# VectorE alone sums the sixteen tiles of expert rows of the first block, one strided reduce for each

## What is computed

```python
x = x + 0.5 * ffn(layernorm(x))
x = x + attn(layernorm(x))
x = x + 0.5 * ffn(layernorm(x))
```

```python
y = jnp.einsum('ecf,edf->ecd', jax.nn.silu(g) * u, down_w)
out = jnp.zeros_like(flat).at[tok_table.reshape(-1)].add((y * w_table[..., None]).reshape(-1, d))
```

## Time and profile before

| | us |
|---|---|
| median of 3 runs | 972.84 (972.01 to 973.99) |
| the profiled execution | 972.94 |
| its span in the trace | 971.2 |

### The profile page before, as it was taken

How to read it: one execution, slowest core, us unless ns; L and a number is a source line. 1 busy time by engine, 2 the same in 40 slices (tenths; PEclk the granted TensorE clock), 3 DMA queues, 4 the chain that set the end, 5 groups by cost and what they waited for, 6 DMA issues and landing times.

```text
span 971.2 us, 18502 instructions
## 1 busy us (share of the span) xinstructions
PE 915.0 (94%) x5770; PEld 561.1 (58%) x5772; DVE 763.6 (79%) x2079; ACT 646.6 (67%) x1426; POOL 645.6 (66%) x607
## 2 busy tenths in 40 slices
PE   4999789999999999999999999999999999978987
PEld 3766466555555555555555555555555555765666
DVE  6954399998888888888888888888878789876247
ACT  5634446877778687777778778777777787543431
POOL 3368778878676868778676766867677455236741
PEclk9999989999999999999999999999999999988999
DMA  8979745666765868797785766756575564485757
GB/s 338 356 247 316 270 163 163 100 136 109 153 129 101 169 151 185 141 223 158 177 192 98 153 104 137 153 103 140 107 151 96 90 120 87 89 334 153 250 204 273
DMA packets 302978, 165.58 MB, mean 170 GB/s; under 512 B 278176, under 2 KB 285600, under 8 KB 300832
## 3 DMA queue, kind: packets, MB, share of 16 engines
q1 hardware_dynamic: 297696, 146.56, 62.7%
q0 software_dynamic: 3072, 9.44, 3.0%
q10 hardware_dynamic: 2112, 8.39, 2.1%
HBM read 68.93 MB, written 28.31 MB: 100 GB/s over the span
## 4 chain that ended last, share of the span: by engine, by line
PE 75%; DVE 13%; DMA 4%; issue 3%; ACT 2%; SPq 1%; another core or an unknown queue 0%; POOL 0%; DVEq 0%; ACTq 0%
PE b_p L110 5%; PE b_o L110 5%; PE b_o L111 5%; PE b_o L112 5%; PE b_p L111 5%; PE b_p L112 5%; PE b_s L110 5%; PE b_s L112 5%; PE b_s L111 5%; PE b_out L110 3%; PE b_out L112 3%; PE b_out L111 3%; PE b_v L110 2%; PE b_v L112 2%; PE b_v L111 2%
## 5 line engine op out<-in xcount | busy, mean ns | idle before, releaser
L2452 POOL TENSOR_TENSOR h<-pr,h 128x512 f16<-128x512 f32 x256 | 293.1, 1158 | 160.6 <-ACT h L1171 155.1
L1161 ACT ACTIVATE pr<-b_s,nmax,kappa 128x512 f32<-128x512 f32 x256 | 197.5, 774 | 41.1 <-DVE nmax L1907 36.7
L1904 DVE TENSOR_SCALAR_CACHE_REDUCE junk<-b_s 128x512 bf16<-128x512 f32 x256 | 175.3, 685 | 22.6 <-PE b_s L112 17.5
L1171 ACT ACTIVATE h<-pr 128x512 f16<-128x512 f32 x256 | 153.3, 626 | 0.7 <-DMA pT<-h 0.4
L1935 DVE SCALAR_TENSOR_TENSOR x<-b_out,rinv,x 128x256 f32<-128x256 f32 x256 | 111.4, 476 | 41.8 <-PE b_out L112 40.3
L110 PE MATMUL b_p<-xh,w 128*128 128x512 f16 x256 | 97.8, 382 | 3.1 <-DVE qT L1846 2.2
L110 PE MATMUL b_o<-pT,v 128*128 128x512 f16 x256 | 97.1, 379 | 1.7 <-DVE oT L1923 1.7
L111 PE MATMUL b_p<-xh,w 128*128 128x512 f16 x256 | 97.8, 382 | 0.0
L110 PE MATMUL b_s<-kT,qT 128*128 128x512 f16 x256 | 97.1, 379 | 0.7 <-ACT pr L1161 0.7
L112 PE MATMUL b_p<-xh,w 128*128 128x512 f16 x256 | 97.6, 381 | 0.0
L111 PE MATMUL b_s<-kT,qT 128*128 128x512 f16 x256 | 97.1, 379 | 0.0
(11 more groups left out here) (223 smaller groups left out, 2234.1 us busy)
## 6 DMA issues: line engine op xcount, KB each, us to landing
raw<-in_experts SPq DMA_DIRECT2D x32, 768.0 KB, 8.0
raw_cs<-in_heads SPq DMA_DIRECT2D x16, 1024.0 KB, 5.2
zrows<-zero ACTq DMA_DIRECT2D x4, 2048.0 KB, 11.5
z<-zrows SPq DMA_DIRECT2D x16, 512.0 KB, 4.2
zrows<-zero SPq DMA_DIRECT2D x16, 512.0 KB, 3.9
zl<-zrows SPq DMA_DIRECT2D x16, 512.0 KB, 8.8
rows<-xn SPq DMA_DIRECT2D x8, 512.0 KB, 10.7
pT<-h SPq DMA_TRANSPOSE x256, 3.2
```

What stands on the lines that cost most here:

```text
L1161: act.activation(pr[n % 4][:], b_s[n % 3][:], ACT.Exp, bias=nmax[:, u % 2, i:i + 1], scale=kappa[:, s:s + 1], accum_out=rsum[:, u % 2, i:i ...
L1171: act.activation(h[n % 4][:, 0, :], pr[n % 4][:], ACT.Copy).then_inc(q["p_high"], 1)
L1904: dve.tensor_scalar(junk[n % 2][:], b_s[n % 3][:], 0.0, None, ALU.add, ALU.max, accum_out=peaks[:, n % 2:n % 2 + 1]).then_inc(q["peak_read ...
L2452: pool.tensor_tensor(h[n % 4][:, 1, :], pr[n % 4][:], h[n % 4][:, 0, :], ALU.subtract).then_inc(q["p_split"], 1)
```

## The change

In the first block `combine` is one `tensor_reduce` over z, read as 256 sums of four elements that lie 256 columns apart, into a free y slot, and the add of it to x. DVE does all sixteen tiles; POOL's `combine` and its two semaphores are gone, and what waited for them waits for DVE's count. The last block's combine stays as it is. All five lists are new up to unit 7 and from unit 56 or 57 on; no call is added or dropped but the sixteen `combine` calls' places. The loop from 8 to 55 is unchanged.

```diff
@@ statistics (DVE)
-                    if C < 6:
-                        dve.wait_ge(q["x_done"], 4 * (C - 4) + 4)
-                    else:
-                        dve.wait_ge(q["xp_done"], 4 * (C - 6) + 4)
+                    dve.wait_ge(q["x_done"], 4 * (C - 4) + 4)
@@ combine (DVE)
-                own.did(dve.tensor_tensor(zi[:, 0:2 * D], zi[:, 0:2 * D], zi[:, 2 * D:4 * D], ALU.add))
-                own.wait()
-                own.did(dve.tensor_tensor(zi[:, 0:D], zi[:, 0:D], zi[:, D:2 * D], ALU.add))
+                if lap == 0:
+                    rows = y[i % 3][:]
+                    own.did(dve.tensor_reduce(rows, zi[:].rearrange("p (k d) -> p d k", k=K), X, ALU.add))
+                else:
+                    rows = zi[:, 0:D]
...
-                dve.tensor_tensor(x[:, i, :], x[:, i, :], zi[:, 0:D], ALU.add).then_inc(q["x_done"], 1)
+                dve.tensor_tensor(x[:, i, :], x[:, i, :], rows, ALU.add).then_inc(q["x_done"], 1)
@@ combine (POOL)
-            def combine(I):
...
-                pool.tensor_tensor(x[:, I, :], x[:, I, :], zi[:, 0:D], ALU.add).then_inc(q["xp_done"], 1)
@@ load_z (SP)
-                if ZS <= I < 8 + ZS:
+                if ZS <= I < NT:
                     sp.wait_ge(q["x_done"], I - ZS + 1)
-                elif 8 + ZS <= I < NT:
-                    sp.wait_ge(q["xp_done"], I - ZS - 7)
```

More of the change, by code:

```diff
@@ L2037, in _ @@
+            combine(7)
+            add_shared(2)
             low(4)
+            statistics(5)
             hidden(14)
-            add_shared(2)
+            queries(0)
             hidden(15)
-            combine(6)
-            queries(0)
             keys_of(0)
-            combine(7)
-            statistics(5)
+            combine(8)
             maxima(0, 0)
             maxima(0, 1)
+            queries(1)
+            maxima(0, 2)
+            combine(9)
+            combine(10)
+            shift(5)
@@ L2048, in _ @@
+            combine(11)
             keys_of(1)
-            queries(1)
-            shift(5)
+            maxima(0, 3)
             values(0)
-            add_shared(3)
-            maxima(0, 2)
-            low(5)
-            maxima(0, 3)
-            maxima(1, 0)
-            values(1)
-            statistics(6)
-            maxima(1, 1)
-            keys_of(2)
-            queries(2)
-            maxima(1, 2)
+            statistics(6)
+            low(5)
+            maxima(1, 0)
+            maxima(1, 1)
@@ L2063, in _ @@
+            values(1)
+            add_shared(3)
+            shift(6)
+            maxima(1, 2)
+            queries(2)
+            keys_of(2)
+            combine(12)
+            combine(13)
+            sums(0)
+            queries(3)
+            maxima(1, 3)
             values(2)
-            sums(0)
-            maxima(1, 3)
+            keys_of(3)
             maxima(2, 0)
-            queries(3)
-            shift(6)
             maxima(2, 1)
-            keys_of(3)
-            sums(1)
@@ L2085, in _ @@
-            statistics(7)
-            sums(2)
-            values(4)
-            maxima(4, 0)
-            add(0, 1)
             outputs(1)
             shift(7)
+            maxima(4, 0)
+            add(0, 0)
+            queries(5)
+            keys_of(5)
+            sums(2)
+            add(0, 1)
+            low(7)
+            values(5)
+            add(1, 0)
             maxima(4, 1)
-            keys_of(5)
-            queries(5)
-            add(1, 0)
-            low(7)
+            queries(6)
@@ L2157, in _ @@
             maxima(56, 1)
+            queries(57)
+            maxima(56, 2)
+            keys_of(57)
+            values(57)
             outputs(54)
-            keys_of(57)
-            maxima(56, 2)
-            queries(57)
-            values(57)
+            queries(58)
             maxima(56, 3)
-            add(54, 0)
             maxima(57, 0)
```

1214 lines of the change are left out of this document (602 added, 612 removed).

## The result

The changed kernel takes 983.0 us (median of 4 runs, 979.43 to 990.3) beside 973.41 for the kernel before, a ratio of 1.0105 with a 95% interval of 1.0072 to 1.0137. It is slower by about 1%; 971.0 was forecast, so the sign was wrong. The profiled run took 979.43 us for a span of 977.7.

A forecast was written before the change was run, and what follows sets the result against it. PE, busy 94% of the span, was taken as the bound, with PE waiting for DVE in the turn to attention. Span 971.2 - 0.4 (turn) - 1.5 (tail) = 969.3, +1.74 gives 971.0 us; range 966 to 986.

The forecast's parts named there:

- The price of the reduce: First block's combine on DVE: strided reduce taken at 1.22 us, bounds 1.22 and 2.41; a tile 1.80 us, sixteen 28.8 us.
- Rival 1: Strided reduce takes 2.2 to 2.4 us, PE waits for every `maxima`: 983 to 987 us, say 985; chance 0.25.
- Contention: DVE beside GpSimd: `tensor_reduce` never contends; without that rule about 3 us over sixteen reduces; add of x 0.50 us.
- Head: Start, up to the first gather: it no longer waits for the weights and comes at about 60.2 instead of 61.67, -1.5 us.
- GpSimd's queue: GpSimd through the experts: queue full, last scatter near 114, combine's first rows at about 119.8 instead of 117.5, +2.3 us.
- The turn: First feed-forward block to attention: `scores(0, 0)` at about 144.5, +1.8 us at `maxima(3, 0)`, `scores(7, 3)` at 233.7, -0.4 us.
- rival 3: Early lead at `scores(0, 0)` is kept: 3 to 5 us of 5.0 stay, 966 to 968 us; chance 0.13.
- The tail: From unit 57 to the end: same work in another order, -1.5 us, between -4 and +2.
- The signs I named: Trace marks: reduces at 1.22 us, `scores(0, 0)` near 147, DVE over 95% busy from 120 to 190, `scores(7, 3)` near 234.

## Why the prediction was wrong

**The price of the reduce: this step failed.** I wrote "I take 1.22: same engine, same count, same type". The three samenesses did not matter; the one difference did, the step between the inputs. It is 1.98 us, between my bounds of 1.22 and 2.41. With 1.22 the time is 968.4, measured, and the sign of my forecast would have been right. The upper one was no bound for DVE either: it was GpSimd's time, and that 1.98 lies under it is luck. I had both ends in the range (966 to 986 holds 983.0) but took the lower end, since it was the row of the same engine; a range from 1.22 to 2.41 with no row in between and a turning point of 1.5 called for more than one chance in four above it.

**Rival 1 came true.** It was to decide from 1.5 us per reduce, with 978 at 1.8 us and 985 at 2.2 to 2.4. At 1.98 that line gives about 980.5; the profiled runs took 979.43 and 979.07, the medians 983.0 and 981.5. Its picture of PE waiting for every `maxima` did not come: PE's long waits are those of the list above, for `hid`, `axn`, `kT` and `pr`. Beside it stood the Trainium skill (Advanced Engine Details and Errata, SBUF Cachelines), which says that a read in another 16-byte line each time pays a penalty. The trace agrees, down to the place of the jump: 1.22 us at a step of 8 bytes, where a line is hit twice, 1.97 at 16, where it is hit once. Its size, which the page does not give, is 0.75 us on 1024 elements. "Against it: no row shows DVE slower than 1.2 ns an element" was an argument from rows that all read contiguously, and so was none.

**Contention.** "`tensor_reduce` never does", after the Trainium skill (SBUF — State Buffer, Who interferes with whom): the sixteen contiguous reduces lie within 1203 to 1219 ns with GpSimd at work beside them, and the eight strided ones beside GpSimd's adds within 1964 to 2056, while adds went from 0.42 to 1.38. The traces agree. The add of x at 0.50 was right (0.49).

**Head.** The first gather was forecast for 60.2. It came at 58.92, because the weights that it had waited 2.50 us for the earlier trace rows hold it no more:

```profile
58.92 1.21 POOL L2395 DMA_INDIRECT xg<-rows,tok_i  x1 [1.05 <-DVE tok_i L1806]
...
114.12 0.97 POOL L2404 DMA_INDIRECT zrows<-y,slot_i  x1 [2.25 <-ACT y L1127]
```

Right in sign. The nine traces with this head have it at 58.4 to 61.5, the four with the old head at 61.0 to 61.7, so the 1.3 us between forecast and trace are no finding.

**GpSimd's queue.** Last scatter forecast near 114, first rows at 119.8; measured 114.12 and 120.29. Right for this trace, though the last scatter waits 2.25 us for ACT's `y`, so it is no longer the full queue that sets it. With the same lists the first rows came at 121.78 with the adds and at 122.15 with the contiguous reduce, 2 us later than forecast.

**The turn.** Forecast for the price of 1.22, so the kernel with the contiguous reduce is its measure. `scores(0, 0)`: 144.5 there and 145.15 measured ("near 147" among the signs was careless). At `scores(3, 0)` that kernel is 3.0 us behind the kernel before (180.5 to 177.5), where I had 1.8 at `maxima(3, 0)`. `scores(7, 3)`: 233.7 forecast, 229.5 measured. I counted that PE is 4.5 us of matmuls further at `scores(3, 0)`, and used it only to say that PE "isn't set back there". Those matmuls need not be done later; from `scores(3, 0)` to `scores(7, 3)` the new order takes 49.1 us and the old 55.9. So the turn was forecast 4 us too pessimistically at `scores(7, 3)`, and 5.8 at `scores(56, 0)`, which that kernel reaches at 738.19, 6.2 us before the kernel before, where I had 0.4. The time is that of rival 3, which I gave 0.13. Its reasons are seen in part: the granted clock from 120 to 185 is 0.97 instead of 0.92, and PE's longest wait 2.7 us instead of 3.8. How much is theirs and how much the order's was not separated.

**The tail.** Forecast -1.5 us, between -4 and +2. Alone it measured +1.7 [+0.4, +3.0]; in the changed kernel 1.0084 with and 1.0066 without it; with adds 0.9961 and 0.9972 with and 0.9998 without. These do not agree on a sign, and they compare runs from different chips. The traces give the part from `scores(56, 0)` to the end (the third chip and the one with added operations left out): 226.4 to 228.3 us in the four with the old tail, 227.5 to 230.6 in the five with the new. The gain of 1.5 us that I forecast is not there; whether the tail costs something or nothing is open.

**The signs I named.** DVE over 95% busy from 120 to 190: 96.9% (67.85 of 70). "PE idle between 150 and 200 over 10 us would mean rival 1" failed as a sign; PE was idle 6.4 us there, for part of the loss lies earlier. "Reduces of 2 us or more" was the one that held.

In sum: 971.0, less 2.6 for what the other parts were mis-sized together (968.4 measured at the assumed price; in spans 5.8 less up to unit 56 and 2.5 more in the tail), plus 13 for the reduce (981.5 on the second chip).

## What to carry to other kernels

Before one strided operation replaces several contiguous ones, look at the step and not at the element count: here a single pass over 1024 f32 elements at a step of 16 bytes or more costs 1.97 us, more than the 1.11 us of the two contiguous adds (0.69 + 0.42) that give the same sums. Where GpSimd works beside them the adds lose that lead: 1.09 + 0.99 us before, and eight tiles either way took the same time. When no row of the trace has the access pattern that you price, and the price decides the sign, the nearest row by engine and type is no better than the far one; hold both open in the chances. Work moved onto an engine that is over 90% busy in its stretch arrives almost one to one in what waits for it, and cutting it into shorter instructions showed no gain above 2 us here, where the sixteen tiles take some 40.

## What the runs showed of the hardware

The jump sits between steps of 8 and 16 bytes, for f32, alike for a reduce's input (1.22 to 1.97 us for 1024 elements), an add's input (0.42 to 0.61 for 256) and its output (0.43 to 0.61). From 16 bytes to 1 kB the time of the reduce stays within 1.87 and 1.97 us.

On the third chip the kernel before was 3.0% longer and the kernel with adds 2.7%. Of the 22.2 us of span between the two traces with adds, 11.1 have arisen by `scores(0, 0)`, none are added up to `scores(56, 0)`, and the rest comes behind it: the time is lost where the experts are, not in the turn or the loop. Windows of 60 to 80 us, first the kernel with adds on the first chip, then the same kernel on the third:

```profile
60.00:80.00 20.00, 17.66 (x178) 11.16 (x181) 8.64 (x28) 10.08 (x33) 15.32 (x16) 1.00 0.76 266
```

```profile
60.00:80.00 20.00, 14.21 (x112) 8.18 (x111) 7.70 (x20) 7.75 (x26) 12.01 (x12) 0.67 0.52 176
```

PE's granted clock is 0.67 there instead of 1.00, so a good part of the stretch ran at 1.2 GHz, and only 112 matmuls were done for 178. PE had been busy 1.38 of the 4 us from 64 to 68 when the clock fell (3.36 on the first chip), and it stood at 0.50 from 68 to 80; the other two traces from that chip show the same fall, to 0.50 from 72 and from 68 us on. From `scores(0, 0)` to `scores(6, 3)` the two traces agree to 0.1 us. PE ran out of work there first; why it did on that chip and not on the others is open.
